# Evicting the first transposed chunk ahead of the last K/V tile's norms, in batches 1 to 3

## What is computed

```
h  = layernorm(x) * (1 + ca) + sa
Xn = layernorm(h) * gamma + beta
Q, K, V = split(Xn @ W_in + b_in)             # each 512 x 512
K, V = rotary(K), rotary(V)
A  = sum over rows of (K / |K|) * (V / |V|)   # one row of 512
Y  = ((0.5 * A + 0.5) * Q) @ W_out + b_out
x  = x + ga * (Y + h)
h  = layernorm(x) * (1 + cb) + sb
x  = x + gb * (relu(h @ W_up) @ W_down + sum(routing weights) * (h @ W_expert))
```

## Time and profile before

| | |
|---|---|
| median of 3 executions | 386.73 us (384.7 to 387.5) |
| profiled execution, whole time | 386.43 us |
| its span, first to last instruction | 384.6 us |
| PE, DVE, ACT, POOL busy | 367.0, 255.4, 166.7, 113.3 us |
| mean granted TensorE clock | 0.982 |

### The profile page before, as it was taken

The page is one execution under the profiler, slowest core; times in us unless marked ns, Lnnn a source line. Parts: engine busy times, 40 slices in busy tenths (PEclk is TensorE's granted clock), DMA queues, the critical chain, the costliest instruction groups (busy, mean ns, idle before and its releaser), DMA issues.

```text
span 384.6 us, 4649 instructions
## 1 busy us (share of the span) xinstructions
PE 367.0 (95%) x1664; PEld 286.9 (75%) x1664; DVE 255.4 (66%) x515; ACT 166.7 (43%) x293; POOL 113.3 (29%) x110
## 2 busy tenths in 40 slices
PE   4997999899997999989999999999999999999996
PEld 0155888678885888868788878888788878887885
DVE  0677799869978488876887559727550855084354
ACT  1337388884427821075314681247114612541210
POOL 0114683276932528425163151910000001000000
PEclk9988899999999899999999999999999999999999
DMA  7995964050030000000000002100200110011002
GB/s 222 378 388 191 348 258 168 0 164 2 2 82 2 0 0 2 27 2 2 0 27 2 0 0 111 28 2 27 82 2 0 55 56 0 0 57 55 2 0 109
DMA packets 10951, 27.42 MB, mean 71 GB/s; under 512 B 1185, under 2 KB 1569, under 8 KB 9777
## 3 DMA queue, kind: packets, MB, share of 16 engines
q1 hardware_dynamic: 10928, 27.13, 19.8%
HBM read 22.90 MB, written 4.23 MB: 71 GB/s over the span
## 4 chain that ended last, share of the span: by engine, by line
PE 66%; DVE 12%; issue 7%; ACT 6%; DMA 4%; POOL 2%; SPq 1%; DVEq 0%; ACTq 0%; POOLq 0%
PE ps L1032 19%; PE ps L1034 19%; PE ps L1033 19%; PE ps L1039 3%; PE ps L1056 2%; DMA xs<-in_wmod 2%; DMA xs<-in_X 2%; ACT sqj L444 2%; DVE hb L657 1%; PE ps L1047 1%; ACT ps L493 1%; DVE ps L690 1%; PE ps L1159 1%; PE ps L1160 1%; ACT t_hi L495 1%
## 5 line engine op out<-in xcount | busy, mean ns | idle before, releaser
L1032 PE MATMUL ps<-w_hi,t_hi 128*128 128x512 f32 x192 | 75.7, 394 | 0.0
L1034 PE MATMUL ps<-w_hi,t_lo 128*128 128x512 f32 x192 | 75.2, 392 | 0.0
L1033 PE MATMUL ps<-w_lo,t_hi 128*128 128x512 f32 x192 | 75.2, 392 | 0.0
L1032 PE MATMUL ps<-t_hi,w_hi 128*128 128x512 f32 x128 | 51.6, 403 | 0.0
L1032 PE MATMUL ps<-w_hi,g_hi 128*128 128x512 f32 (+1 forms) x132 | 51.3, 389 | 0.3 <-DVE g_lo L743 0.3
L1034 PE MATMUL ps<-w_hi,g_lo 128*128 128x512 f32 (+1 forms) x132 | 50.6, 383 | 0.0
L1033 PE MATMUL ps<-w_lo,g_hi 128*128 128x512 f32 (+1 forms) x132 | 50.5, 383 | 0.0
L1034 PE MATMUL ps<-t_hi,w_lo 128*128 128x512 f32 x128 | 50.4, 393 | 0.0
L1033 PE MATMUL ps<-t_lo,w_hi 128*128 128x512 f32 x128 | 50.4, 393 | 0.0
L683 DVE TENSOR_TENSOR t_lo<-ps,t_hi 128x512 fp32r<-128x512 f32 x32 | 21.8, 688 | 32.9 <-ACT t_hi L495 32.6
L1032 PEld LDWEIGHTS ps<-w_hi,t_hi 128*128 128x128 f32 x192 | 36.5, 190 | 7.6
(11 more groups left out here) (130 smaller groups left out, 613.8 us busy)
## 6 DMA issues: line engine op xcount, KB each, us to landing
xs<-in_X SPq DMA_DIRECT2D x4, 1024.0 KB, 7.5
stage<-in_w SPq DMA_DIRECT2D x4, 1024.0 KB, 6.8
out<-xs SPq DMA_DIRECT2D x15, 256.0 KB, 2.0
xs<-in_wmod SPq DMA_DIRECT2D x3, 1024.0 KB, 9.8
xs<-in_wmod SPq DMA_DIRECT2D x8, 256.0 KB, 7.0
stage<-in_w SPq DMA_DIRECT2D x8, 256.0 KB, 9.6
gate_bc<-mod_rows SPq DMA_DIRECT2D x8, 256.0 KB, 6.7
gate_bc<-in_wmod SPq DMA_DIRECT2D x1, 1024.0 KB, 11.9
```

The lines of the kernel that those rows point to most:

```text
L1032: mm(dst, l_hi, r_hi, start=start, stop=False)
L1033: mm(dst, l_hi, r_lo, start=False, stop=False)
L1034: return mm(dst, l_lo, r_hi, start=False, stop=stop)
```

## The change

On ScalarE, in batches 1 to 3, `t_evac(b + 1, 0)` moves ahead of `norm_sums(b, 3)`. On VectorE, in the same batches, `t_split(b + 1, 0)` moves ahead of `kv_products(b, 3)`. Batch 0 keeps its order, and so do the lists of TensorE, GpSimd and the DMA queues.

```diff
--- before.py
+++ after.py
@@ -545,10 +545,12 @@
                     normalise(b + 1, 2, 2)
                 else:
                     normalise(B, 0, NT)
+                if b > 0:
+                    t_evac(b + 1, 0)
                 norm_sums(b, 3)
                 if b == B - 1:
                     split_hi(5)
-                for c in range(NC):
+                for c in range(1 if b > 0 else 0, NC):
                     t_evac(b + 1, c)
                 if b + 2 < B:
                     normalise_x(b + 2)
@@ -832,8 +834,11 @@
                     x_shift(b + 2)
                 kv_sum(b, 2)
                 kv_rows(b, 3)
+                if b > 0:
+                    t_split(b + 1, 0)
                 kv_products(b, 3)
-                t_split(b + 1, 0)
+                if b == 0:
+                    t_split(b + 1, 0)
                 t_split(b + 1, 1)
                 kv_sum(b, 3)
                 a_pairs(b)
```

## The result

| | us | runs |
|---|---|---|
| before, median | 386.42 (383.96 to 388.0) | 20 |
| changed kernel, median | 388.28 (385.39 to 389.98) | 20 |
| ratio | 1.0053, 95% interval 1.0033 to 1.0074 | |
| changed kernel, span of the profiled execution | 386.6 (before 384.6) | |

The change makes the kernel 0.5% slower. 388.5 was forecast, with +2.06 against the kernel before; +1.86 was measured between the medians, +2.0 between the two spans.

What follows compares the result with a forecast made beforehand. TensorE, busy 367.0 of 384.6 us, was taken as the bound, so only its pauses and clock could move time: -0.87 - 1.57 - 0.39 + 3.32 + 1.57 = +2.06 on 386.43 gives 388.5 us, range 385.8 to 390.4.

Steps and rivals of the forecast that it cites:

- batch 1, pauses: Batch 1, TensorE: pause before chunk 2's transposes gone, chunk 3's transposes start at 122.75 instead of 123.62; 0.87 us won.
- batch 1, clock: Batch 1, from chunk 3's transposes to the first small sum: clock holds at full instead of falling; 1.57 us won.
- batch 2, pauses: Batch 2, TensorE: chunk 3's transposes start at 172.94 instead of 173.33; 0.39 us won.
- batch 3, pause: Batch 3: norms and expert-weight split queue ahead of chunk 1's eviction; chunk 3's transposes at 223.24 instead of 219.92; 3.32 us lost.
- batch 3, clock: Batch 3: clock falls behind TensorE's pause of about 2.8 us; bounds 0 and 1.57, taken 1.57 us lost.
- What is late next: Batch 1: chunk 1's low part, after the products end at 122.01; larger second pause gives back nearly half a microsecond.
- The rival that rested on the Trainium skill: Batch 3: the clock holds there too, the fall being a draw; sum +0.49, 386.9 us; chance 0.20.

Runs made afterwards that it cites:

- both chunks first: Against the kernel before, batches 1 and 2 evict and split chunks 0 and 1 ahead of tile 3's norms and products; batch 3 unchanged: 386.38 us, ratio 1.0000.

## Why the prediction was right, step by step

| step | forecast | measured, from chunk 0's transposes on |
|---|---|---|
| batch 1, pauses | -0.87 | -0.94 (5.51 against 6.45) |
| batch 1, clock | -1.57 | -1.57 against the first profile of before, 0 against the second |
| batch 2, pauses | -0.39 | -0.43 |
| batch 3, pause | +3.32 | +3.20 (7.25 against 4.05) |
| batch 3, clock | +1.57 | +1.44 (4.70 against 3.26 up to the small sums) |
| sum | +2.06 | +1.70 |

The spans differ by 2.0; the missing 0.3 are a term that I left out. In batch 2 the stretch is 48.01 against 48.14, though 0.43 was won in it. From batch 1's small sums to batch 2's first transposes it takes 39.30 instead of 39.01, and on the way a weight load of TensorE stands idle before a group of output rows, for the low part of the gated Q:

```profile
134.48 0.19 PEld L1037 LDWEIGHTS ps<-w_hi,g_hi 128*128 128x128 f32 x1 [0.44 <-DVE g_lo L745]
```

This wait was not there before. It goes with a VectorE product ahead of it that took 1.31 instead of 0.98: of the 14 profiles, the seven in which that product took 1.29 or more have the wait (0.42 to 0.45), and the seven in which it took 0.98 or less have none. The change in batch 1 alone, with the same order of work up to there, drew the short one, 0.16, and took 38.98. The last section says what is known of the product.

- **The pause of batch 3** was forecast within 0.12, and its parts are shown: taking the split from ahead of chunk 1 took 1.8 of it away.
- **The pauses of batches 1 and 2** hold to 0.07. "What is late next" was right: chunk 1's low part, by products that start behind chunk 0's. With both chunks first the wait appears at the small sums.
- **The clock of batch 1** is where the working was weaker than the number. I took 1.57 as won, since the profile at hand had the fall. The second profile of the kernel before has the same pauses and no fall. So the 1.57 was a draw of that one profile, and in a median it counts for a part: about 1.2, by the estimate from the mean clocks. The rival that rested on the Trainium skill, "TensorE: Matmul & The Clock Gate", section "What's actually happening" (a monitor that runs free of the kernel's start), named this. The repeated profiles agree with it: equal pauses, and the clock fell once and held once, in two kernels. My reason for the draw's outcome, that the clock holds behind shorter pauses and falls behind longer ones, did not stand: it fell behind 1.35 and held behind 0.78 and 1.79, and once behind 1.53 and 1.30.
- **The clock of batch 3** fell in three of three profiles with a pause of 3.0. It does not in every execution: in 2 of the 20 the mean clock leaves no room for it.
- That the median came out 0.2 from the forecast is partly luck. The sum of the pauses is not: +2.06 forecast, +2.12 measured with the left-out wait, and 1.9 between the medians at equal clock. The clock stood in the sum twice, with the same 1.57 and opposite signs, so that taking both falls as certain cancelled. Had only one place had such a term, the forecast would have been off by what was overstated.

## What to carry to other kernels

When an instruction is moved ahead on an in-order engine, ask of each place whether what it now waits for comes later than the work that it jumps over. Here the same edit won where that work filled time in which the eviction was ready, and lost where it had filled idle time. It was worth doing in batch 1. In batch 2 the pauses shrank by 0.4, but most of that went into the wait that the long product brought, and the times of batch 1 alone and of batches 1 and 2 (384.27 and 383.90 on the same chip) are too close to tell apart. And a pause can have a second price in the clock, which one profile shows as if it were certain: profile twice, compare stretches between fixed points of the program, not spans, and look at the mean granted clock of every timed execution.

## What the runs showed of the hardware that I had not expected

A VectorE product of four columns, `ab_col` (L739, L741), takes anything between 0.16 and 1.33 us. Where it is long, it runs while GpSimd adds 128x512 rows, and it ends when one of those ends. In the changed kernel:

```profile
127.10 1.31 DVE L741 TENSOR_TENSOR ab_col<-a_col,col 128x4 f32<-128x4 f32 x1
```

```profile
124.61 5.03 POOL L356 TENSOR_TENSOR hb<-hb,bo_bc 128x512 f32<-128x512 f32 x4 [2.70 <-DVE pair L734]
```

GpSimd's four additions are about 1.26 apart, so the third ends near 128.39; the product ends at 128.41. In the first profile of the kernel before the product runs from 129.62 to 130.60, and the last addition ends at 130.58. In the second, GpSimd starts at 126.72, its second addition ends near 129.23, and the product that starts at 129.20 takes 0.16. The closest pair is the changed kernel and the change in batch 1 alone, which have the same work here:

```profile
126.86 0.16 DVE L741 TENSOR_TENSOR ab_col<-a_col,col 128x4 f32<-128x4 f32 x1
```

```profile
124.39 5.04 POOL L356 TENSOR_TENSOR hb<-hb,bo_bc 128x512 f32<-128x512 f32 x4 [2.71 <-DVE pair L734]
```

There the product starts 2.47 behind GpSimd's first addition and takes 0.16; in the changed kernel it starts 2.49 behind it and takes 1.31. In both the second addition ends near 2.52. With both chunks first it starts 1.93 behind, takes 0.60, and ends with the second addition. So an operation on four columns can cost over a microsecond by its phase against GpSimd's work. No experiment moved GpSimd's work on purpose, so why one waits for the other is argued from these coincidences and not shown.
